# Constant products among the potentials' products of a fused decoder layer on one Trainium2 core

## What is computed

```python
xn1 = layernorm(x, ln1_g, ln1_b)
pot = xn1 @ w_pot + b_pot
V = pot[..., 0]
gamma = jax.nn.softplus(pot[..., 1]) + GAMMA_FLOOR
bk_features = bk_core_diag(V, gamma)
x = x + bk_features @ w_bk + b_bk
```

## Time and profile before

| | us |
|---|---|
| Median of 3 runs | 768.02 |
| Lowest and highest | 767.54, 770.93 |
| The profiled execution, its whole time | 772.6 |
| Its span in the profile | 770.7 |
| PE busy | 658.1 (85%) |
| DVE busy | 505.1 (66%) |
| ACT busy | 400.8 (52%) |
| POOL busy | 321.6 (42%) |

### The profile page before, as it was taken

How to read it: one execution, slowest core, us unless ns; L and a number is a source line. 1 busy time by engine, 2 the same in 40 slices (tenths; PEclk the granted TensorE clock), 3 DMA queues, 4 the chain that set the end, 5 groups by cost and what they waited for, 6 DMA issues and landing times.

```text
span 770.7 us, 19904 instructions
## 1 busy us (share of the span) xinstructions
PE 658.1 (85%) x6190; PEld 495.3 (64%) x6190; DVE 505.1 (66%) x1733; ACT 400.8 (52%) x855; POOL 321.6 (42%) x463
## 2 busy tenths in 40 slices
PE   9879898899998998998999989985867999999920
PEld 8664756755755754764764764763643999999920
DVE  4587568768678669668668678774525555545535
ACT  0212365474475375475475565553420777767716
POOL 6104362363354264264165156145014355544535
PEclk7579999999999999999999999996558999999975
DMA  8600000000000000000000000000023322222144
GB/s 286 220 1 14 2 30 16 2 25 14 4 25 14 4 23 13 7 21 14 7 21 11 11 12 20 11 0 29 2 110 90 78 74 73 72 64 68 54 166 180
DMA packets 26058, 36.23 MB, mean 47 GB/s; under 512 B 7302, under 2 KB 18311, under 8 KB 25736
## 3 DMA queue, kind: packets, MB, share of 16 engines
q1 hardware_dynamic: 20582, 22.72, 9.6%
q0 software_dynamic: 4576, 9.53, 3.6%
q10 hardware_dynamic: 850, 3.38, 1.3%
HBM read 23.99 MB, written 12.63 MB: 48 GB/s over the span
## 4 chain that ended last, share of the span: by engine, by line
PE 51%; DVE 15%; issue 12%; POOL 9%; ACT 6%; DMA 2%; SPq 1%; DVEq 1%; ACTq 1%; POOLq 0%
PE bank L1561 9%; PE bank L1876 8%; PE bank L1886 7%; PE bank L1726 4%; POOL rstd L737 4%; ACT mix L555 3%; PE bank L1597 3%; PE bank L1713 3%; PE bank L1695 3%; PE bank L1645 2%; PE bank L1653 2%; PE bank L1484 2%; POOL vare L734 1%; PE bank L1734 1%; POOL expert_in L779 1%
## 5 line engine op out<-in xcount | busy, mean ns | idle before, releaser
L779 POOL DMA_INDIRECT expert_in<-xb_rows,slot_u x72 | 73.3, 1018 | 102.5 <-PE bank L1704 48.9
L871 POOL DMA_INDIRECT expert_out<-xa,v_sb x71 | 68.5, 965 | 79.3 <-issue 43.0
L675 ACT ACTIVATE hT<-bank,qT 128x128 f32<-128x128 f32 x284 | 81.2, 369 | 38.0 <-PE bank L1876 20.3
L734 POOL TENSOR_SCALAR vare<-mv 128x1 f32<-128x1 f32 (+1 forms) x108 | 23.9, 221 | 168.2 <-DVE mv L1064 167.8
L1186 DVE TENSOR_REDUCE negmax<-bank 128x4 f32<-128x512 f32 x128 | 79.4, 683 | 8.6 <-PE bank L1695 8.6
L555 ACT ACTIVATE mix<-bank 128x512 f32<-128x512 f32 x128 | 66.1, 604 | 23.4 <-PE bank L1713 23.4
L1886 PE MATMUL bank<-w_t,hT 128*128 x568 | 75.8, 276 | 1.6 <-ACT hT L675 0.6
L1876 PE MATMUL bank<-xnT,qT 128*128 128x128 f32 x568 | 75.2, 275 | 1.1 <-DVE qT L1400 1.1
L1886 PEld LDWEIGHTS bank<-w_t,hT 128*128 128x128 f32 x568 | 69.1, 192 | 2.8 <-issue 2.5
L737 POOL TENSOR_TENSOR rstd<-vare,minus_half 128x1 f32<-128x1 f32 (+1 forms) x108 | 66.5, 615 | 9.6 <-POOL vare L734 1.2
L1876 PEld LDWEIGHTS bank<-xnT,qT 128*128 128x128 f32 x568 | 69.0, 192 | 1.6 <-DVE qT L1400 1.6
(11 more groups left out here) (300 smaller groups left out, 1461.4 us busy)
## 6 DMA issues: line engine op xcount, KB each, us to landing
v_sb<-expert_in SPq DMA_DIRECT2D x71, 66.0 KB
w_t<-in_w_t ACTq DMA_DIRECT2D x1, 2064.0 KB, 7.4
x_all<-in_x SPq DMA_DIRECT2D x4, 512.0 KB, 7.9
xT_all<-in_xT SPq DMA_DIRECT2D x4, 512.0 KB, 8.6
ctxT<-in_ctxT SPq DMA_DIRECT2D x8, 256.0 KB
w_t<-in_w_t SPq DMA_DIRECT2D x1, 2048.0 KB, 7.4
x_all<-expert_out SPq DMA_DIRECT2D x4, 512.0 KB, 10.0
mix<-expert_out SPq DMA_DIRECT2D x3, 512.0 KB, 7.2
```

The source lines that it names most:

```text
L675: ins = nc.scalar.activation(hx[j % 2][:, c, :], bank[2 + j % 2][:, c * P:(c + 1) * P], ACT.Gelu, bias=w1c[j % 2][:, FF + c:FF + c + 1])
L779: nc.gpsimd.indirect_dma_start(xs[:, :], bass.IndirectOffsetOnAxis(ap=slot_u[:, t, k:k + 1], axis=0), xb_rows[k][:, t, :], None).then_inc( ...
L871: nc.gpsimd.indirect_dma_start(ys[:, :], bass.IndirectOffsetOnAxis(ap=tag[j % ROWS][:, HOME - P:HOME - P + 1].bitcast(U32), axis=0), ysb[j ...
```

## The change

`potentials` no longer issues one constant product ahead of each call, but one ahead of every second product, behind the wait for the input's quarter. Three constant products are put behind the wait for the small loads and ahead of the mean's product, and two behind the mean's product. Twelve constant products are added among the potentials (16 in place of 4), and five around the small products. Nothing else changes; the constant products still write to bank 7 and nobody reads them.

```diff
             def potentials(q):
-                fill(1)
                 pe.wait_ge(xT_loaded[q], 16)
                 for n in range(8 * q, 8 * q + 8):
+                    if n % 2 == 0:
+                        fill(1)
                     ins = mm(bank[4][:, 2 * n:2 * n + 2], xT_all[:, n * P:(n + 1) * P], w_potc[:, :],
                              start=True, stop=True)
                 ins.then_inc(zpos_mm, 1)
@@
             pe.wait_ge(ones_ready, 2)
             fill(25)
             pe.wait_ge(pot_loaded, 16 * len(POT_LOADS))
+            fill(3)
             pe.wait_ge(ones_ready, 2)
             pe.wait_ge(wpotg_ready, 1)
             mm(bank[2][:, 0:2], mean_w[:, :], w_potg[:, :], start=True, stop=True).then_inc(wmean_mm, 1)
+            fill(2)
             pe.wait_ge(lnb_ready, 1)
```

## The result

The changed kernel takes 773.37 us (median of 6 runs, 771.33 to 777.24), the kernel before 767.78 us (6 runs). The ratio is 1.0077, with a 95% interval of 1.0048 to 1.0107: slower by 0.8%, 5.6 us.

A forecast was written before the change was run, and what follows sets the result against it. The end of TensorE's potentials was taken to bound the scan's start. With a held clock, -3.0 us there and -0.2 us at the `drow` records gave -3.2 us, so 764.8 us on the median, range 762.5 to 771.5.

The forecast's parts named there:

- What bounds the kernel: Start of the kernel: the end of the potentials sets the scan's start; every microsecond there reaches the end unless something else is due.
- rival 3: Potentials: the clock holds but a late `xT_all` quarter or POOL's `rstd` is due, 766 to 767 us; chance 0.05.
- The cost of a product: TensorE's products, wide or narrow: 0.427 us each at clock 0.50 and 0.223 us at 1.00, a gap of 0.204 us.
- Part 1: Small products ahead of the potentials: three and two added constant products cost 0.6 us; the row starts at 10.78, before 10.19.
- Does the clock hold?: Potentials' row: one wide product in three holds the clock at 1.00 throughout, giving 764.8 us; chance 0.50.
- The closed gap: Ahead of the mean's product: the idle gap from 8.6 to 9.37 is filled, which was counted in favour of holding the clock.
- The break-even at 18.2: Potentials' row: the change pays only if the clock holds for 33 of 48 products, until 18.2.
- rival 2: Potentials: the clock falls early, between 11.4 and 14.8; the row ends 3.1 to 6.2 us later, 771.1 to 774.2; chance 0.20.
- rival 1: Potentials: no gain, the clock falls between 17 and 19.5 and 19 to 9 products run slowly, about 768.0 us; chance 0.25.
- the sum of the row: Potentials: 48 products at 0.223 us take 10.7 us from 10.78, last slot ending at 21.5, so `zpot` comes 3.0 us sooner.

The follow-up runs named there:

- e3: The kernel before with the four constant products among the potentials left out, nothing else changed: 758.65 us against 759.91, ratio 0.9985.
- e4: The changed kernel with a constant product ahead of every potential, 64 products in the row: 761.62 us against 759.91 for the kernel before.
- e7: The changed kernel with constant products ahead of two of every three potentials, 22 in all: 760.09 us against 759.81 for the kernel before.
- e9: The changed kernel with one 256-column bf16 constant product ahead of each potential instead, and five pairs fewer in the scan: 755.90 us against 760.42 before.
- e1: The kernel before with only the five constant products around the small ones added: 761.43 us against 759.91, ratio 1.0020.
- e10: The kernel before with the five constant products around the small ones added and none among the potentials: 758.75 us against 760.42, ratio 0.9974.
- e2: The kernel before with only the constant product ahead of every second potential, nothing around the small products: 767.83 us against 759.91, ratio 1.0091.
- e12: The changed kernel again, unchanged, for a third profile: ratio 1.0068 to the kernel before, from 2 runs of the changed kernel.

## Why the prediction was wrong, point by point

- **What bounds the kernel** was right: what was lost at `zpot` was lost at the end of the scan (2.18 and 2.16 us), and in e3, e4 and e7 to e9 as well `zpot` went where the row of potentials went. PE had no gap in the row, and DVE waited for it last: no quarter of `xT_all` and no `rstd` held it up (rival 3).
- **The cost of a product** was right: three products took 0.67 us at 1.00 and 1.28 us at 0.50. With the measured start (11.14) and fall (16.6), 24.5 products run fast and 23.5 slowly, which gives 11.14 + 5.46 + 23.5 x 0.427 = 26.6; the last narrow row ends at 26.85 (26.00 + 0.85).
- **Part 1** was put at 0.6 us, and this term was too small. In the profile the row started at 11.14 and not at 10.78. One half of the 0.36 us is that the mean's product started at 9.85 and not at 9.67, because the constant products of the start ended later, which depends on the execution. The other half is that the two products for `pot_bias` took 0.31 us each (10.52, 10.83, 11.14) and not 0.223. And where the clock falls at a given moment, each microsecond of delay ahead of the row moves its end by 0.427 / 0.223 = 1.9 us, since fewer products come before the fall. e1 starts its row 0.96 us later than before (11.15 against 10.19), 1.8 us by this sum; it measured 1.5 us, with an interval from 0.1 to 3.
- **Does the clock hold?** This is the step that failed, and with it the sign. The row against holding that I gave, 1.06 us of wide records in the 3.4 us ahead of the fall at 526.8 against 1.1 us in the new mixture, pointed the right way. I set against it that PE and the weight loads are busy throughout. The runs show that this isn't enough: PE was busy without a gap in the row of each of these kernels, and the clock fell at 15.7 to 17.4 with 16 wide products (three profiles) and held to the row's end with 22 and with 32 (one profile each). So the forecast of 3.2 us less became 5.6 us more.
- **The closed gap** I took as an argument for holding. e1, e3 and e10 show the clock falling at 13.2 to 13.8 with the gap closed or open, and at the same 13.2 where the start was alike (e1, e3: 43 records). What the small part does is to let the first microseconds of the mixture pass: without it the changed row loses the clock at 12.3 (e2), with it at 15.7 after a like start (e12), and up to 17.4.
- **The break-even at 18.2** was right and is what decides: all three falls of the changed kernel lie ahead of it. Of the rivals, 2 (slower) came nearest, but not by its bounds: it had the fall ahead of 14.8, and rival 1 had it from 17 on (with 19 slow products from there, where the sum gives 20), so two of the three falls (15.7, 16.6) lie between them and one (17.4) in rival 1. That the measured 773.4 lies within rival 2's 771.1 to 774.2 is luck. By the break-even alone, falls at 15.7 to 17.4 cost 0.7 to 2.3 us (4.5 products x 0.204 for each microsecond); with the measured starts (10.91 to 11.54) the sum gives 2.1, 2.1 and 2.5 us behind the first profile of before, and the three `zpot` lie 2.18, 2.18 and 2.59 behind it. So the sum of the row was right once its start and the fall are known.
- **What is left.** The medians differ by 5.6 us on the first chip (interval 3.7 to 8.2), 3.6 (2.9 to 6.6) and 4.7 (3.3 to 7.1) on the others. Between like starts the row of potentials gives 3.3 us measured and 4.0 estimated. That lies within these intervals on two chips, and on the first at their lower end. Whether something else adds 1 to 2 us there is open: the profiles show no second place that the change moves, and the last group's spread of 6 us could hide one.

## What to carry to other kernels

Work that is put in only to keep TensorE's clock has a break-even: count how many products must still run fast for the longer row to pay, and find a row of the trace at which a similar mixture held. A busy engine is no sign that the clock holds: here it went with how many of the products were wide. A delay ahead of such a row costs more than its own length if the clock falls at a given moment (here 1.9 times). And before two profiles are compared, check that their clock came up alike. If constant products are needed, take a form whose columns run beside the next weight load (here one bf16 product of 256 columns, +0.03 us each) and not one that pays for its own weights (an fp32 product, +0.223 us), and look for queues of constant products that run past what waits behind them.

## What was not expected of the hardware

- A row with TensorE and its weight loads busy all the time lost the clock within 2 to 6 us of its start (e2, and the changed kernel), when only every third fp32 product was 128 columns wide and the others were 2. With 22 wide ones beside 32 it was kept.
- The clock rises and falls at other moments in each execution of one program, by 0.8 us in before's potentials (11.4 to 12.2) and by 1.7 us in the changed kernel's (15.7 to 17.4). In the last group it came back within the stretch from 550 to 560 us in one execution and not in another, and the stretch up to the experts took 71.0 or 77.1 us. How many of the first constant products were done by 8.50 us told when the clock would fall in the row.
